# Attention over tokens with heads packed into TensorE's row and column groups of 32

## The reference

```python
def mha_bchw(x, qkv_w, proj_w, proj_b):
    B, C, H, W = x.shape                      # C = 64, H * W = 256 tokens
    hd = C // HEADS                           # 8 heads of 8 channels
    t = x.reshape(B, C, H * W).transpose(0, 2, 1)
    qkv = (t @ qkv_w.T).reshape(B, H * W, 3, HEADS, hd).transpose(2, 0, 3, 1, 4)
    q, k, v = (qkv[0], qkv[1], qkv[2])
    attn = jax.nn.softmax(jnp.einsum('bhnd,bhmd->bhnm', q, k) * hd ** (-0.5), axis=-1)
    o = jnp.einsum('bhnm,bhmd->bhnd', attn, v).transpose(0, 2, 1, 3).reshape(B, H * W, C)
    o = o @ proj_w.T + proj_b
    return o.transpose(0, 2, 1).reshape(B, C, H, W)
```

## Time and profile before

| | |
|---|---|
| median of 3 runs | 2453.7 us (2452.26 to 2458.58) |
| profiled execution | 2455.15 us, span of the trace 2453.3 us |
| busy of the span | TensorE 87%, VectorE 76%, ScalarE 58%, GpSimd 58% |
| mean granted clock of TensorE | 0.941 |
| attention stage, L2180 to L2221 | from 223.06 and from 1421.41 us |

### The profile page before, as it was taken

The page is one execution under the profiler, slowest core; times in us unless marked ns, Lnnn a source line. Parts: engine busy times, 40 slices in busy tenths (PEclk is TensorE's granted clock), DMA queues, the critical chain, the costliest instruction groups (busy, mean ns, idle before and its releaser), DMA issues. The chain is left out here.

```text
span 2453.3 us, 28912 instructions
## 1 busy us (share of the span) xinstructions
PE 2144.5 (87%) x7243; PEld 1122.6 (46%) x7243; DVE 1864.1 (76%) x3251; ACT 1434.4 (58%) x2268; POOL 1412.1 (58%) x1287
## 2 busy tenths in 40 slices
PE   2998869898998999997988987698979799999798
PEld 2397635443453444433335964353435334444243
DVE  6556767589986999995755668565999589999754
ACT  1843444286884777773346446335868567777632
POOL 2232008488977999982322400393989399999532
PEclk9989989999998999998997998799999899999899
DMA  5000192500001222225810005634000012212344
GB/s 188 1 1 1 48 339 82 176 39 0 1 1 23 43 44 57 44 52 161 232 41 0 1 0 195 215 106 166 1 1 1 11 22 44 61 39 56 91 119 114
DMA packets 199338, 172.76 MB, mean 70 GB/s; under 512 B 72535, under 2 KB 175327, under 8 KB 195831
## 3 DMA queue, kind: packets, MB, share of 16 engines
q1 hardware_dynamic: 199159, 170.78, 24.3%
HBM read 81.69 MB, written 72.29 MB: 63 GB/s over the span
## 5 line engine op out<-in xcount | busy, mean ns | idle before, releaser
L942 POOL TENSOR_TENSOR BIG<-BIG 128x512 f32<-128x512 f32 x320 | 407.1, 1272 | 91.9 <-DVE BIG L850 73.5
L850 DVE TENSOR_TENSOR BIG<-PSUM,BIG 128x512 f32<-128x512 f32 x576 | 390.8, 681 | 61.0 <-PE PSUM L1061 35.5
L1133 DVE SCALAR_TENSOR_TENSOR PSUM<-BIG,VECS,PSUM 128x1024 f32<-128x1024 f32 x224 | 288.2, 1286 | 37.0 <-PE PSUM L2112 31.8
L776 POOL TENSOR_TENSOR BIG<-TOEP,BIG 128x384 f32<-128x384 f32 x84 | 98.0, 1194 | 320.2 <-DVEq L1558 320.2
L1069 PE MATMUL PSUM<-BIG,CSTS 128*128 128x512 f32 x512 | 264.9, 598 | 0.0
L2112 PE MATMUL PSUM<-BIG,WDW 128*128 128x512 f32 x512 | 233.0, 599 | 13.8 <-ACT BIG L2012 13.8
L1061 PE MATMUL PSUM<-BIG,SELB 120*128 120x512 bf16 x576 | 210.6, 384 | 16.9 <-issue 10.1
L2291 PE MATMUL PSUM<-BIG 128*128 128x381 f32 (+1 forms) x576 | 189.4, 492 | 12.9 <-DVE BIG L783 12.9
L1061 PEld LDWEIGHTS PSUM<-BIG,SELB 120*128 120x128 bf16 x576 | 55.1, 96 | 262.0 <-DVE BIG L850 163.3
L2112 PEld LDWEIGHTS PSUM<-BIG,WDW 128*128 128x128 f32 x512 | 97.1, 192 | 141.0 <-issue 115.0
L1785 POOL TENSOR_TENSOR BIG<-BIG 128x1024 f32<-128x1024 f32 x64 | 151.0, 2360 | 10.3 <-POOL BIG L1788 10.3
(11 more groups left out here) (365 smaller groups left out, 5170.9 us busy)
## 6 DMA issues: line engine op xcount, KB each, us to landing
spill<-X SPq DMA_DIRECT2D x18, 1024.0 KB, 5.9
back_spill<-BIG SPq DMA_DIRECT2D x32, 576.0 KB, 3.4
X<-x SPq DMA_DIRECT2D x32, 512.0 KB, 7.9
rows_spill<-X SPq DMA_DIRECT2D x64, 256.0 KB, 4.0
out<-BIG SPq DMA_DIRECT2D x64, 256.0 KB, 3.6
BIG<-rows_spill SPq DMA_DIRECT2D x28, 512.0 KB, 5.2
X<-back_spill SPq DMA_DIRECT2D x14, 896.0 KB, 11.7
BIG<-fc SPq DMA_DIRECT2D x8, 1024.0 KB, 10.3
```

Source lines behind the costliest of these rows:

```text
L776: eng.tensor_tensor(to.rearrange("p (x c r) -> p x c r", x=3, r=WROW), TOEP[:, y].unsqueeze(1).unsqueeze(1).broadcast_to([P, 3, WCH, WROW] ...
L850: dve.tensor_tensor(img(product_buffer(b, q)), img(PSUM[:, (k + q) % 2, :]), pch(c, XBASE, dy, dx), ALU.mult).then_inc(df_p, 1)
L942: pool.tensor_tensor(a, a, x, ALU.add).then_inc(df_add, 1)
L1133: return dve.scalar_tensor_tensor(out=rows8(to), in0=strip(c, base, dy, dx), scalar=vc(weights, j), in1=rows8(acc), op0=ALU.mult, op1=ALU.add)
```

## The change

The 16 heads are taken as 4 groups of 32 partitions (g) with 4 heads in each (j). Head (g, j) has the channels 32 g + 8 j onward.

- `QM` is now four copies of Q, copy j with the rows of the heads (0..3, j) kept and the others zero. ScalarE makes them right out of PSUM, with a mask as its scale, `COL4`, which VectorE computes once at the start. `VM` is four such copies of V. GpSimd makes them, by products with `HEAD4`, four matrices of ones and zeros that it writes in each pass.
- A step is still two heads, but neighbouring groups g of the same j. Their logits products use only the 32 rows of their group (`rows(g)`), for the two heads in turn, each into its own bank.
- The exponentials have no accumulator, and the weights are not normalised. VectorE's reciprocal and L1437 go.
- Transposes stay as they were, 8 a step, but the copies to `PTB` are shared: VectorE takes the even head, ScalarE the odd one. `PTB` has 8 places, `PB` 4.
- After every second step `values(j)` multiplies four heads: for both key halves, with V (bank 7) and with `HEAD4` (bank 6), four products with 32 weight columns, each into the 32 PSUM partitions of its group. Bank 6 then holds each head's sum of weights on the 8 rows of the head.
- At the end VectorE takes the reciprocal of bank 6 and multiplies bank 7 with it: `OB`. ScalarE's copy and the products with zeros go.
- The steps are written out, 8 in a row, with no hardware loop inside. A semaphore counts once for two heads, not for each. The new tiles lie in `BIG` from its first column on, where the padded image stood in the stages before.

The diff, cut to its core (the removed steps stand above in the kernel):

```diff
         r.at = both
-        SFC, QB, KB, OB = (r.take(TOK) for _ in range(4))
+        SFC, KB, OB = (r.take(TOK) for _ in range(3))
         VB = r.take(2, P)
-        QM = r.take(2, TOK)
-        PB = [r.take(2, 2, TOK), REG[:, both - 4 * TW * TW - TOK:both - 4 * TW * TW - TOK + 4 * TOK].rearrange(
-            "p (k h n) -> p k h n", k=2, h=2)]
-        assert 4 * TW * TW + TOK >= 4 * TOK
-        PTB = r.take(2, 2, TOK)
-        VM = r.take(2, 2, P)
-        MHS = r.take(2, 6)
+        MHS = r.take(4, 4)
+        QM = BIG[:, 0:4 * TOK].rearrange("p (j n) -> p j n", j=4)
+        VM = BIG[:, 4 * TOK:8 * TOK].rearrange("p (j k n) -> p j k n", j=4, k=2)
+        HEAD4 = BIG[:, 8 * TOK:10 * TOK].rearrange("p (j n) -> p j n", j=4)
+        PB = BIG[:, 10 * TOK:18 * TOK].rearrange("p (n q k) -> p n q k", n=4, q=2)
+        PTB = BIG[:, 18 * TOK:34 * TOK].rearrange("p (n k q) -> p n k q", n=8, k=2)
+        INVS = BIG[:, 34 * TOK:35 * TOK]
+        COL4 = SM[:, 48:52]
...
+        def turned(n):
+            return PSUM[:, 4 + n % 2, :].rearrange("p (a b) -> p a b", a=2)
...
+            dve.tensor_reduce(COL4, cs("headcol").rearrange("p (g j) -> p j g", j=4), AX.X, ALU.add)
...
-                in_turn(dve, NH // 2, 2, 1, step)
+                def largest(s):
+                    dve.wait_ge(mh_s, pair * HSTEPS + (s + 1))
+                    for k in range(2):
+                        g = 2 * (s % 2) + k
+                        ins = dve.tensor_reduce(MHS[:, g, 0:2], PSUM[:, g, :].rearrange("p (a b) -> p a b", a=2), AX.X, ALU.max)
+                    ins.then_inc(mh_mx, 1)
+                    dve.wait_ge(mh_mx, pair * HSTEPS + (s + 1))
+                    two = slice(2 * (s % 2), 2 * (s % 2) + 2)
+                    dve.tensor_scalar(MHS[:, two, 2:4], MHS[:, two, 0:2], -HD ** -0.5, None, ALU.mult).then_inc(mh_nmx, 1)
+                largest(0)
+                largest(1)
+                for s in range(HSTEPS):
+                    n = 2 * s
+                    dve.wait_ge(mh_pt, pair * HSTEPS + (s + 1))
+                    if n >= 8:
+                        dve.wait_ge(mh_pv, pair * 4 + ((n - 8) // 4 + 1))
+                    dve.tensor_copy(PTB[:, n % 8, :, :], turned(n)).then_inc(mh_ptd, 1)
+                    if s + 2 < HSTEPS:
+                        largest(s + 2)
+                dve.wait_ge(mh_pv, pair * 4 + 4)
+                dve.reciprocal(INVS, PSUM[:, 6, 0:TOK]).then_inc(mh_out, 1)
+                dve.wait_ge(mh_out, pair * 2 + 1)
+                dve.tensor_tensor(OB, PSUM[:, 7, 0:TOK], INVS, ALU.mult).then_inc(mh_out, 1)
+                dve.wait_ge(mha_pe, pair * 2 + 2)
...
+                pool.wait_ge(mha_act, pair + 1)
+                settle(pool)
+                pool.memset(HEAD4, 0.0).then_inc(mh_head, 1)
+                pool.wait_ge(mh_head, pair * 2 + 1)
+                settle(pool)
+                for j in range(4):
+                    ins = pool.memset(HEAD4[:, j, :].rearrange("p (g i c) -> p g i c", i=4, c=HD)[:, :, j, :], 1.0)
+                ins.then_inc(mh_head, 1)
+                pool.wait_ge(mh_head, pair * 2 + 2)
+                settle(pool)
+                for j in range(4):
+                    pool.tensor_tensor(VM[:, j, :, :], VB, HEAD4[:, j, :].unsqueeze(1).broadcast_to([P, 2, P]),
+                                       ALU.mult).then_inc(mh_vm, 1)
...
-                act.activation(QB, PSUM[:, 0, 0:TOK], ACT.Copy)
...
-                in_turn(act, NH // 2, 1, 1, step)
-                act.wait_ge(mha_pe, pair * 3 + 2)
-                act.activation(OB, PSUM[:, 7, 0:TOK], ACT.Copy).then_inc(mha_act, 1)
+                act.wait_ge(mha_pe, pair * 2 + 1)
+                act.activation(KB, PSUM[:, 7, TOK:2 * TOK], ACT.Copy)
+                act.activation(QM[:, 0, :], PSUM[:, 7, 0:TOK], ACT.Copy, scale=COL4[:, 0:1]).then_inc(mh_qm, 1)
+                act.activation(VB, PSUM[:, 6, 0:2 * P].rearrange("p (a b) -> p a b", a=2), ACT.Copy).then_inc(mha_act, 1)
+                for j in range(1, 4):
+                    act.activation(QM[:, j, :], PSUM[:, 7, 0:TOK], ACT.Copy, scale=COL4[:, j:j + 1]).then_inc(mh_qm, 1)
+                def weigh(s):
+                    act.wait_ge(mh_nmx, pair * HSTEPS + (s + 1))
+                    if s >= 2:
+                        act.wait_ge(mh_pt, pair * HSTEPS + (s - 1))
+                    for k in range(2):
+                        g = 2 * (s % 2) + k
+                        for q in range(2):
+                            ins = act.activation(PB[:, g, q, :], PSUM[:, g, q * TOK:(q + 1) * TOK], ACT.Exp,
+                                                 bias=MHS[:, g, 2 + q:3 + q], scale=HD ** -0.5)
+                    ins.then_inc(mh_exp, 1)
+                weigh(0)
+                for s in range(HSTEPS):
+                    if s + 1 < HSTEPS:
+                        weigh(s + 1)
+                    n = 2 * s + 1
+                    act.wait_ge(mh_pt, pair * HSTEPS + (s + 1))
+                    if n >= 8:
+                        act.wait_ge(mh_pv, pair * 4 + ((n - 8) // 4 + 1))
+                    act.activation(PTB[:, n % 8, :, :], turned(n), ACT.Copy).then_inc(mh_pta, 1)
...
-                pe.matmul(PSUM[:, 7, 0:TOK], cs("zero"), SFC, start=True, stop=False, skip_group_check=True)
...
-                in_turn(pe, NH // 2, 1, 1, step)
-                pe.matmul(PSUM[:, 7, 0:TOK], cs("zero"), KB, start=False, stop=True,
-                          skip_group_check=True).then_inc(mha_pe, 1)
...
+                def rows(g):
+                    return slice(g * 32, (g + 1) * 32)
+                def logits(s):
+                    pe.wait_ge(mh_qm, pair * 4 + (s // 2 + 1))
+                    if s >= 2:
+                        pe.wait_ge(mh_exp, pair * HSTEPS + (s - 1))
+                    settle(pe)
+                    for q in range(2):
                         for k in range(2):
+                            g = 2 * (s % 2) + k
+                            ins = pe.matmul(PSUM[:, g, q * TOK:(q + 1) * TOK], QM[rows(g), s // 2, q * P:(q + 1) * P],
+                                            KB[rows(g), :], start=True, stop=True)
+                    ins.then_inc(mh_s, 1)
+                def turn_heads(s):
+                    pe.wait_ge(mh_exp, pair * HSTEPS + (s + 1))
+                    if s >= 1:
+                        pe.wait_ge(mh_pta, pair * HSTEPS + s)
+                        pe.wait_ge(mh_ptd, pair * HSTEPS + s)
+                    for k in range(2):
+                        n, g = 2 * s + k, 2 * (s % 2) + k
+                        for h in range(2):
+                            for q in range(2):
+                                ins = pe.transpose(PSUM[:, 4 + n % 2, (h * 2 + q) * P:(h * 2 + q + 1) * P],
+                                                   PB[:, g, q, h * P:(h + 1) * P], ident)
+                    ins.then_inc(mh_pt, 1)
+                def values(j):
+                    pe.wait_ge(mh_pta, pair * HSTEPS + (2 * j + 2))
+                    pe.wait_ge(mh_ptd, pair * HSTEPS + (2 * j + 2))
+                    pe.wait_ge(mh_vm, pair * 4 + (j + 1))
+                    pe.wait_ge(mh_qm, pair * 4 + 4)
+                    settle(pe)
+                    for h in range(2):
+                        for w, bank in ((VM[:, j, h, :], 7), (HEAD4[:, j, :], 6)):
+                            for g in range(4):
+                                ins = pe.matmul(PSUM[rows(g), bank, 0:TOK], w[:, rows(g)], PTB[:, (4 * j + g) % 8, h, :],
+                                                start=(j == 0 and h == 0), stop=(j == 3 and h == 1))
+                    ins.then_inc(mh_pv, 1)
+                logits(0)
+                logits(1)
+                for s in range(HSTEPS):
+                    turn_heads(s)
+                    if s + 2 < HSTEPS:
+                        logits(s + 2)
+                    if s >= 2 and s % 2 == 0:
+                        values(s // 2 - 1)
+                values(3)
+                pe.wait_ge(mh_out, pair * 2 + 2)
```

More of the change, by code:

```diff
@@ L26 @@
 NH = 2 * HEADS
+HSTEPS = NH // 2
 GROUP = 4
@@ L339, in program @@
         mha_pe, mha_act = sem("mha_pe"), sem("mha_act")
-        mh_qm, mh_s, mh_mx, mh_nmx, mh_exp, mh_rec, mh_pn, mh_pt, mh_ptc, mh_vm, mh_pv = steps(
-            "mh_qm", "mh_s", "mh_mx", "mh_nmx", "mh_exp", "mh_rec", "mh_pn", "mh_pt", "mh_ptc", "mh_vm", "mh_pv")
+        mh_qm, mh_s, mh_mx, mh_nmx, mh_exp, mh_out, mh_head, mh_pt, mh_pta, mh_ptd, mh_vm, mh_pv = steps(
+            "mh_qm", "mh_s", "mh_mx", "mh_nmx", "mh_exp", "mh_out", "mh_head", "mh_pt", "mh_pta", "mh_ptd", "mh_vm", "mh_pv")
         so_dve, so_pe = sem("so_dve"), sem("so_pe")
@@ L1901, in _ @@
                 in_turn(act, NS // 2, 1, 0, step)
-                act.wait_ge(mha_pe, pair * 3 + 1)
-                act.activation(QB, PSUM[:, 0, 0:TOK], ACT.Copy)
-                act.activation(KB, PSUM[:, 0, TOK:2 * TOK], ACT.Copy)
```

(27 more changed lines are left out.)

71 lines of the change are left out of this document (2 added, 69 removed).

## The result

The changed kernel takes 2433.5 us (2429.5 to 2444.8, 7 runs), the kernel before 2453.2 us in the same comparison: a ratio of 0.9918 with a 95% interval of 0.9898 to 0.9939. It is faster by 19.7 us, where 30.7 were forecast; the time lies in the range of 2412 to 2446 us, but not in the 2415 to 2430 that the forecast had for its own case.

What follows compares the result with a forecast made beforehand. TensorE and VectorE were taken to bound the attention stage nearly equally. Passes of 50.1 and 51.6 us falling to 35.5 each save 30.7: 2455.15 becomes 2424.4, less 1.45 to the median 2423 us; range 2412 to 2446.

Steps and rivals of the forecast that it cites:

- its own case: Whole kernel: packing works in full by rows and columns, 2423 us, within 2415 to 2430; chance 0.65.
- rival (a): Attention stage: row groups go one after the other, 2435 us, or column groups by two, 2437; chance 0.17.
- rival (d): Attention stage: clock stays at 1.2 GHz throughout, 54.7 us a pass, 2461 us; chance 0.02.
- Its own sign of being wrong: Changed stage: value groups over 3.5 us, gaps between forms well over 0.2, or the clock falling inside the stage.
- TensorE and VectorE bound it nearly equally: Old attention stage, middle 40 us: TensorE busy 34.3 us and VectorE 32.1, so relieving one alone would bring little.
- 1.73 us for a value group: Values and sums for four heads: 32 records, four column groups side by side, against 6.91 us one after the other.
- 0.88 us for a logits group: Logits of a step: 8 records on two alternating row groups, limited by weight loads of 0.110, against 1.73 us in turn.
- Changes of form: TensorE between kinds of work: the array refills at 0.21 us each, five times per two steps, 1.0 us.
- The further tail of 0.16 us at each change: TensorE at about 20 changes a pass: an exposed record tail would make the time some 6.5 us longer.
- 1.0 us a pass: Attention stage: added to 34.5 us because TensorE waits longer in the thin first steps and the clock may fall.
- my schedule: First pass: first transposes at 230.6, transposes(6) at 248.1, projection at 257.5, 34.5 us in all.
- the range's lower end of 2412: Whole kernel: form changes cost nothing and the clock does not fall, 33.3 us a pass, with shorter exponentials.

Runs made afterwards that it cites:

- experiment 8: The kernel before, with its normalising product on VectorE cut from 512 to 2 columns: 2449.1 us, ratio 0.9983.
- experiment 9: The kernel of experiment 5 with three more full-array products in TensorE's pause before the Q product: 2424.9 us, ratio 0.9883.
- experiment 5: The changed kernel with two full-array products in each of TensorE's two early pauses, after the second and fourth logits groups: 2421.0 us, ratio 0.9869.
- experiment 6: The changed kernel with all logits products on the same 32 rows (0 to 31): 2456.8 us, ratio 1.0013.
- experiment 10: The kernel of experiment 5 with its fill products on 32 rows instead of 128: 2442.1 us, ratio 0.9957.
- experiment 4: The changed kernel with logits products on all 128 rows instead of the 32 of their group: 2432.6 us, ratio 0.9918.
- experiment 1: The changed kernel with two full-array products between the second logits group and the first transposes only: 2433.3 us, ratio 0.9911.
- experiment 11: The changed kernel as it is, run again on the same chip as the kernel of experiment 5: 2436.8 us, ratio 0.9928.

## Why the prediction was right, and where it failed

**In short.** The work was priced nearly right, and the change was faster for the reasons given. The clock was not, and that the time still fell into the range is partly luck: the range reached to 2446 us to take in rival (a), packing that works by half, at 2435. Packing worked in full, and the time came out at 2433.5 by a clock at half speed for the first part of the stage, which the prediction had as rival (d) and gave 0.02. Its own sign of being wrong, that the clock falls inside the stage, came in.

**What bounds.** That the stage stands alone and passes its gain to the span held: 18.9 of 21.6 us. That TensorE and VectorE bound it nearly equally did not hold for the steady step: experiment 8 took over 1 us of VectorE's work out of it and the step stayed at 4.92. The sum did not rest on that, since both got less work; that relief of VectorE alone would bring little was right.

**Columns.** The step from two column groups to four held, and so did 1.73 us for a value group: 1.87 from start to start. By the Trainium skill's figure ("TensorE: Matmul & The Clock Gate", Part 3: 3.07x for four tiles by rows) the estimate was 2.25 us; the measurement is shorter, 4.0 times with tails taken off.

**Rows.** 0.88 us for a logits group was nearly right at full clock: 1.06 from start to start. The reason given, weight loads at 0.110 us a record, is not the limit (experiment 9 has at most 0.08); 0.107, half of 0.216, is what two row groups side by side give. At half clock the first sixteen records, on all four row groups, take 2.23 us where I had 3.4 for two groups.

**Changes of form.** Forecast 1.0 us per two steps. The groups' starts give 2 x 1.02 + 2 x 1.06 + 1.87 = 6.03 against pitches of 5.25: 0.8 us, 0.16 a change. The further tail of 0.16 us at each change, which would have made the time 6.5 us longer, is not there.

**VectorE, ScalarE, GpSimd.** No bound at full clock, as said. The four exponentials take 1.57 us, inside 1.3 to 1.9; I took the low end. GpSimd's products end at 229.2, ahead of the first value group at 241.93. The tail of reciprocal (1.76) and product (0.42) came as priced.

**The clock: the term that was mis-sized.** I allowed 1.0 us a pass for it. From transposes(0) to transposes(3) the changed kernel takes 15.3 and 14.6 us, experiment 5 takes 9.8 and 9.9 with all of it at 1.00, and a fill in it. That is 5.5 and 4.7 us, against 2.0 allowed. The rest are smaller: the first transposes come 0.9 and 0.4 us later than forecast, the same stretch at 1.00 takes 9.8 where my schedule had 9.1, and from transposes(3) to the projection it is 18.5 and 18.1 us where it had 17.8. Rival (d) was the right mechanism, for a part of the stage. Its refusal was the step that failed: I argued from L2260, where the clock rose during packed products, but those use all 128 rows, and the changed kernel's logits behind the first two groups use 64 at a time. The value groups, packed like L2260, did see the clock rise in both passes. The row was read for more than it showed. A small slip beside it: the range's lower end of 2412 is not its parts, since 33.3 us a pass gives 2419 and the rest was left to exponentials without a price.

**The cause of the low clock**, then, as far as the runs show it: with transposes and products on 32 rows TensorE stayed at 1.2 GHz even with no pause in 23.9 us (experiment 6), and fill on 32 rows did nothing (experiment 10). With logits on 128 rows (experiment 4) or fill on 128 rows in both pauses (experiment 5) it was at 2.4 GHz from the first transposes on; with one pause filled it rose and fell again (experiment 1). Once there, the steps with value groups held it. The transposes use all 128 rows and did not raise the clock in experiments 6 and 10, so the rows of ordinary products are what the runs tell of. Whether transposes alone would hold it was not tried, nor products on 64 rows alone: L2096 has 64 rows and ran its 7.89 us at 1.00, but there the clock was at 1.00 already, through 4.88 us without work before it.

**Not followed.** The other stages move by a few us from kernel to kernel with their own clock: the span outside the two stages was 2351.6 us before, 2348.9 in the changed kernel, 2352.4 in experiment 1, 2347.3 in 5 and 2353.3 in 9, and 2356.4 when the changed kernel was traced again (experiment 11). So a few us of any total here are not the stage's; one kernel alone differs by 7.5 us there from execution to execution.

## What to carry to other kernels

Packing small products into row and column groups shortens them as counted, and the order of issue hardly matters; but price the clock as well as the work, since products on few rows left it at half here. Where they stand in a thin beginning, put full-array products into TensorE's pauses, or leave the first groups unpacked (experiment 4 left all of them; the first alone were not tried), and look at the granted clock of the stage and not only at its busy time. And where a row of the trace stands for an instruction not yet seen, name what differs, rows as well as columns, before taking its behaviour over.

## What the runs showed of the hardware

- Four column groups of 32 ran nearly four times as fast as the full width with float32 products of 256 columns: 1.93 against 7.17 us for 32 records.
- Two row groups ran side by side at full clock (8 records in 1.13 us, against 1.99 on one row group and 1.89 on all rows), and four at either clock (16 records in 2.23 us at 0.50 and 1.29 us at 1.00).
- Products on different groups need not keep program order: exchanging loops changed 1.93 to 1.97 us, and in experiment 10 the fill started between logits records that stand ahead of it. The Trainium skill ("TensorE: Matmul & The Clock Gate", Part 3, what overlaps and what doesn't) has products strictly in order in start and end; here the measurement says otherwise for products on row or column groups that differ.
- The granted clock stayed at 0.50 over 23.9 us of unbroken work on 32 rows and transposes, and was 1.00 from the first transposes on with as many products on 128 rows (experiment 4).
